# A graph network's last stage: the bias of each tile's normalisation formed on GpSimd instead of VectorE

## What is computed

```python
def _layernorm(x, axis=-1, eps=1e-05):
    m = jnp.mean(x, axis=axis, keepdims=True)
    v = jnp.var(x, axis=axis, keepdims=True)
    return (x - m) / jnp.sqrt(v + eps)
...
        out = node_feat + out
        mean = out.mean(axis=0)
        var = jnp.mean(jnp.square(out - mean), axis=0)
        out = (out - mean) * jax.lax.rsqrt(var + EPS) * gamma + beta
        return out
...
    x = _layernorm(x + _L1_gnn_ref(x, edge_attr_512, src, dst, ...), axis=-1)
```

## Time and profile before

| | us |
|---|---|
| median of 3 runs | 1352.58 (1351.42 to 1354.11) |
| span of the profiled execution | 1351.3 |
| GpSimd's first gather of the last stage starts | 1206.03 |
| gather 11 / gather 78 (the last) start | 1226.25 / 1336.43 |
| last normalisation starts with two others at | 1347.08 |

### The profile page before, as it was taken

The page is one execution under the profiler, slowest core; times in us unless marked ns, Lnnn a source line. Parts: engine busy times, 40 slices in busy tenths (PEclk is TensorE's granted clock), DMA queues, the critical chain, the costliest instruction groups (busy, mean ns, idle before and its releaser), DMA issues. The chain is left out here.

```text
span 1351.3 us, 21818 instructions
## 1 busy us (share of the span) xinstructions
PE 1282.1 (95%) x6374; PEld 1029.1 (76%) x6374; DVE 1075.9 (80%) x2074; ACT 638.2 (47%) x1243; POOL 817.3 (60%) x752
## 2 busy tenths in 40 slices
PE   7989989999999699999999999999999999979887
PEld 5768768888888588888888888888888888754333
DVE  6577649999999225888889988888888888977887
ACT  3576637888888212333233223322332233257777
POOL 3667346776765542566655666666666565467775
PEclk9999989999999799999999999999999999879999
DMA  8889767888885514444444344444444443759886
GB/s 279 287 280 297 259 203 261 255 257 276 259 261 188 187 47 110 141 131 129 97 135 128 127 126 131 139 135 137 133 140 140 140 140 94 258 175 368 272 283 228
DMA packets 128299, 257.93 MB, mean 191 GB/s; under 512 B 21459, under 2 KB 21907, under 8 KB 128114
## 3 DMA queue, kind: packets, MB, share of 16 engines
q1 hardware_dynamic: 97490, 175.31, 39.8%
q0 software_dynamic: 29920, 80.38, 20.6%
q10 hardware_dynamic: 832, 1.57, 0.3%
HBM read 197.18 MB, written 73.60 MB: 200 GB/s over the span
## 5 line engine op out<-in xcount | busy, mean ns | idle before, releaser
L208 PE MATMUL ps<-w_lo,w_hi 128*128 128x512 f32 (+2 forms) x1140 | 416.3, 365 | 3.6 <-DVE w_lo L1430 1.4
L210 PE MATMUL ps<-w_hi 128*128 128x512 f32 (+2 forms) x1140 | 410.7, 360 | 0.0
L209 PE MATMUL ps<-w_hi,w_lo 128*128 128x512 f32 (+2 forms) x1140 | 410.2, 360 | 0.0
L208 PEld LDWEIGHTS ps<-w_lo,w_hi 128*128 128x128 f32 x1140 | 217.5, 191 | 36.1 <-DVE w_lo L1512 1.9
L210 PEld LDWEIGHTS ps<-w_hi 128*128 128x128 f32 x1140 | 217.0, 190 | 32.4
L209 PEld LDWEIGHTS ps<-w_hi,w_lo 128*128 128x128 f32 x1140 | 217.8, 191 | 29.8
L1268 POOL TENSOR_TENSOR acc_x<-acc_x,node_rows 128x512 f32<-128x512 f32 x72 | 114.8, 1594 | 85.8 <-DMA node_rows<-x_table 81.5
L923 POOL TENSOR_TENSOR node_y<-node_z,node_x 128x512 f32<-128x512 f32 x79 | 102.7, 1300 | 74.0 <-DVE node_agg L1021 39.5
L208 PE MATMUL ps<-w_lo,agg_hi 128*128 128x512 f32 x316 | 132.8, 420 | 1.1 <-DVE agg_lo L992 1.1
L210 PE MATMUL ps<-w_hi,agg_hi 128*128 128x512 f32 x316 | 125.7, 398 | 0.0
L209 PE MATMUL ps<-w_hi,agg_lo 128*128 128x512 f32 x316 | 125.2, 396 | 0.0
(11 more groups left out here) (271 smaller groups left out, 2878.7 us busy)
## 6 DMA issues: line engine op xcount, KB each, us to landing
node_x<-in_x SPq DMA_DIRECT2D x79, 256.0 KB, 4.1
x_table<-node_x SPq DMA_DIRECT2D x79, 256.0 KB, 2.4
node_rows<-x_table SPq DMA_DIRECT2D x79, 256.0 KB, 8.4
coef_all<-coef_table SPq DMA_DIRECT2D x38, 512.0 KB, 7.6
edge_part<-part SPq DMA_DIRECT2D x40, 256.0 KB, 4.4
out_dram<-rows_over_w_lo SPq DMA_DIRECT2D x40, 256.0 KB, 5.7
node_x<-in_ea SPq DMA_DIRECT2D x38, 256.0 KB, 4.3
msg_table<-dst_rows_and_msg SPq DMA_DIRECT2D x38, 256.0 KB, 5.0
```

The source lines that it names most:

```text
L208: pe.matmul(to, left[0], right[1], start=first, stop=False, skip_group_check=onto)
L209: pe.matmul(to, left[1], right[0], start=False, stop=False, skip_group_check=onto)
L210: return pe.matmul(to, left[0], right[0], start=False, stop=last, skip_group_check=onto)
```

## The change

VectorE no longer forms the biases. GpSimd does, in a new third part of its loop: in step k, behind gather k and the multiplication of tile k - 4, it forms both biases of the pair that ends with tile k - 10 (`SHIFT` = 10). It raises a semaphore of its own, `bias_ok`, by one for each tile, and ScalarE's normalisation waits for that instead of `scale_ok`, which VectorE now raises only for the reciprocals. `pair_ends` is the test for the end of a pair, taken out into a function.

```diff
-    PAIR, NORM = 8, 11
+    PAIR, SHIFT, NORM = 8, 10, 11
...
+        def pair_ends(j):
+            return 0 <= j < NT and (j % 2 == 1 or j == NT - 1)
...
-        for k in range(NT + LATE):
+        for k in range(NT + SHIFT):
...
             j = k - LATE
-            if j >= 0 and by_pool(j):
+            if 0 <= j < NT and by_pool(j):
...
+            j = k - SHIFT
+            if pair_ends(j):
+                m, n = j // 2 * 2 % RM, j % 2 + 1
+                pool.wait_ge(scale_ok, j // 2 + 1)
+                for i in range(m, m + n):
+                    nc.gpsimd.tensor_scalar(bias[:, i, :], mv[:, i, 0:1], rstd[:, i, :], -1.0, ALU.mult, ALU.mult).then_inc(bias_ok, 1)
...
-                act.wait_ge(scale_ok, 3 * (j // 2) + 2 + j % 2)
+                act.wait_ge(bias_ok, j + 1)
...
-            if pair:
-                dve.wait_ge(scale_ok, done // 2 * 3 + 1)
-                for i in range(m, m + n):
-                    v.tensor_scalar(bias[:, i, :], mv[:, i, 0:1], rstd[:, i, :], -1.0, ALU.mult, ALU.mult).then_inc(scale_ok, 1)
```

More of the change, by code:

```diff
@@ L1894, in finish_stage @@
         u_before = [landed(NT - 1 - s, 0, 0, 4) for s in range(4)] + [32 * ET // 4] * 2 + [32 * NB // 2] * 2
-        us_ok, pool_ok, sum_ok, stat_ok, root_ok, scale_ok, norm_ok = (sem(n) for n in (
-            "fin_u_scaled_in_psum", "fin_u_scaled_by_pool", "fin_y_summed", "fin_stat", "fin_root_ok", "fin_scale_ok", "fin_norm"))
+        us_ok, pool_ok, sum_ok, stat_ok, root_ok, scale_ok, bias_ok, norm_ok = (sem(n) for n in (
+            "fin_u_scaled_in_psum", "fin_u_scaled_by_pool", "fin_y_summed", "fin_stat", "fin_root_ok", "fin_scale_ok", "fin_bias_ok", "fin_norm"))
+        def pair_ends(j):
+            return 0 <= j < NT and (j % 2 == 1 or j == NT - 1)
         open_ok = g.open_ok
@@ L2081, in vector_program @@
             done = k - PAIRED
-            pair = 0 <= done < NT and (done % 2 == 1 or done == NT - 1)
-            m, n = done // 2 * 2 % RM, done % 2 + 1
-            if pair:
+            if pair_ends(done):
+                m, n = done // 2 * 2 % RM, done % 2 + 1
                 dve.wait_ge(root_ok, done // 2 + 1)
```

## The result

The changed kernel takes 1429.41 us (median of 4 runs, 1428.20 to 1432.74), the kernel before 1352.26 us (4 runs): a ratio of 1.0565, with a 95% interval of 1.0547 to 1.0583. It is 5.65% slower. The forecast was 1423.5 us, with a range of 1405 to 1438.

The account below looks back on a forecast made before the run. The prediction took GpSimd, near its packed pace, to bound the last stage, and a new mutual wait with ScalarE to decide: 70.4 us of loop + 0.5 at the end on 1352.6 gives 1423.5 us, range 1405 to 1438.

Parts of the forecast that it names:

- What bounds the kernel: Last stage: GpSimd runs within 2.5% of its packed pace, 110.18 us for 67 tiles against a floor of 107.5.
- Part 1: VectorE loses 79 operations, 12.7 us; counted as nothing on the path, at the very best 2.7 us.
- Part 2: GpSimd gains 79 operations of one element per partition, two after each gather of an odd step, 0.30 us each.
- d: Time of one small bias operation on GpSimd, taken as 0.30 us; 0.40 by the Trainium skill's ratio.
- Part 3: Odd steps: ScalarE's normalisation waits for a bias behind gather k, which waits for ScalarE's copy; +70.4 us.
- The two pairs of steps: Time from gather k to gather k + 2: 4.52 + d us without a multiplication, 5.65 + d with one.
- The rival of the cheaper handover: Same loop, but a gap of 0.30 us instead of 0.81 from copy to gather: 1406 us, chance 8%.
- the clock costs nothing in the middle: At TensorE's low clock, nine products take 6.9 us, less than the 10.8 us of four tiles in the loop.
- the load rival: Normalisation doesn't wait for gather k, so no loop; GpSimd bound by its load: +15 us, 1368 us, chance 4%.
- The end: From gather 78 to the end of the last normalisation, now 12.75 us: 0 to 2 us more, 0.5 taken.
- the upper bound: The 2 us at the end of the stage, expected if TensorE has fallen to its low clock by then.
- The sum: 70.4 us in the loop + 0.5 at the end = 70.9 us, added to 1352.6: 1423.5 us, 5.2% slower.

Follow-up runs that it names:

- load_alone: Kernel before, biases still on VectorE, plus two small GpSimd operations on a spare tile behind every second gather, nobody waiting for them: 1361.4 us.
- no_mult: Kernel before with all multiplications on VectorE, none on GpSimd: 1351.1 us.
- pool_eighth: Kernel before with one tile of eight multiplied on GpSimd instead of one of four: 1352.1 us.
- no_bias: Kernel before with the 79 biases left out; the normalisation takes a constant: 1351.2 us.
- load_and_wait: Kernel before, biases still on VectorE, plus two small GpSimd operations behind every second gather, for which ScalarE's normalisation also waits: 1427.7 us.
- bias_first: Changed kernel with the two biases of a step ahead of its gather instead of behind it: 1384.1 us.
- shift9: Changed kernel with SHIFT set from 10 to 9, so a pair's biases stand behind the gather and multiplication of the even step before: 1383.3 us.
- two_more_ahead: Changed kernel with two more small GpSimd operations at each pair, between the gather and the first bias: 1444.8 us.
- two_more_behind: Changed kernel with two more small GpSimd operations at each pair, behind the second bias: 1431.8 us.
- last_on_vector: Changed kernel with the biases of tiles 66 to 78 staying on VectorE: 1421.3 us.
- pair_no_mult: Kernel before with one VectorE operation for the two biases of a pair and all multiplications on VectorE: 1349.9 us.

## Why the prediction was right, point by point

**What bounds the kernel.** GpSimd near its packed pace: read rightly from its timeline, and load_alone confirms that load on it has a price, 11.6 us. That it alone sets the pace was too strong, as no_mult and pool_eighth showed. The prediction didn't need more than the first half.

**Part 1, VectorE's relief counts as nothing.** Right: 0.14% at best in no_bias, nothing in load_and_wait.

**Part 2, the price of the operation.** d was taken as 0.30 us, the trace has 0.270. The estimate of 0.40 by the Trainium skill's ratio (GPSIMD Engine Reference, section on performance versus the Vector engine) was further off: here the ratio to VectorE's 0.202 us is 1.34, not 1.96. For this operation of one element a ratio measured on long ones was no guide; the short copies of the earlier trace rows were.

**Part 3, the wait makes a loop.** Right, and shown by five runs: the place of the biases is worth 47 us (bias_first, shift9), two operations cost 15.4 us on one side of the biases and 0.1 us on the other (two_more_ahead, two_more_behind), and the operations with the wait reproduce the change without any relief of VectorE (load_and_wait). The two pairs of steps took 4.84 and 5.97 us for 4.82 and 5.95. For the whole stretch 180.6 us were forecast and 182.39 measured. The difference has these terms: gathers of the even steps take 1.05 us, not 1.00 (33 x 0.05 = 1.6 us), and one gather, at 1353.11, starts 1.1 us late. The smaller d gives 34 x 0.03 = 1.0 us back. The rival of the cheaper handover is out, since it is 0.81 or 0.82 us in every turn of the loop. That the clock costs nothing in the middle was right too: a turn has the same length at 0.70 and at 0.99. Three details were off. The idle time in front of the gathers of even steps was put at some 1.5 us and is 1.90, where the prediction's own terms give 3.22 + 0.30 - 1.04 - 0.03 - 0.60 = 1.85. The normalisations' waits for the bias are 35, not 40. And the load rival took it that a bias ahead of gather k would leave no loop; bias_first still has one, through gather k - 1, and takes 1384 us instead of 1368.

**The end.** This term was mis-sized: 0.5 us taken, at most 2 allowed, and 5.0 us measured (19.89 against 14.87). It has two parts. The last normalisation starts 2.1 us later behind gather 78 than before, just past the upper bound (1423.33 - 1410.61 and three normalisations in 2.10, 14.82 us against 12.75). The step that failed is that VectorE would have the statistics of those tiles done by then. Normalisation 68 starts 2.63 us behind gather 78, not 0.57 (2.4 forecast), and VectorE's statistics of tile 73 start at 4.19 us, not 2.12, because VectorE's multiplication of tile 75 stands in front of them and waits for the bank that normalisation 68 frees. The delay of 2.1 us then stays to the last tile. It is not the clock, which the prediction made the condition for the upper bound: in load_and_wait the granted clock is 1.00 over these 12.8 us, and the last normalisation starts 12.77 us behind gather 78, where the changed kernel has 12.72.

The other 2.9 us stand at the end of the program, which the prediction hadn't looked at: GpSimd's closing `DRAIN`, hidden before. last_on_vector takes 4.5 of these 5.0 us back.

**The sum.** 70.9 us were forecast; the medians differ by 77.2 us, the profiled spans by 79.2. Of the 79.2 us, 72.2 are in the loop and 5.0 at the end. The remaining 2.0 lie ahead of gather 11, of which 1.75 ahead of gather 0, where the two programs have the same instructions; in the other runs gather 0 starts anywhere from 1200.0 to 1210.3 us. The prediction set the profiled span 1.3 us under the median; the runs of the changed kernel show 2.1 to 2.2 us between an execution's time and its span, so the profile of before was likely one of its slower runs. That changes nothing in the difference.

**No version beats both.** pair_no_mult has the lowest median of the complete kernels, 0.15% under the kernel before, with an interval that includes no change.

## What to carry to other kernels

When a step moves to another engine, write down what stands ahead of it in that engine's order, and what that waits for in turn. Here the bias stood behind a gather that waited for a copy on the very engine that waited for the bias, and 20 us of small operations became 72 us of turn-taking. Loads say nothing about this: in the profile both engines have idle time, and each names the other as the one that ended it. The distance in steps between a producer and its consumer is worth checking before what the operation itself costs: one step of distance was worth 47 us, the operations 12. No run tried a distance at which the loop is gone altogether.

## What the runs showed of the hardware

An operation of VectorE that reads two tensors from SBUF (128x2, two operands) can take 1.90 us instead of 0.14 when GpSimd multiplies 128x512 in SBUF, and ends with it. The Trainium skill, SBUF — State Buffer, section on the two separate sides, describes an exclusive lock on a pair of ports that such operations share with GpSimd, which goes to whichever starts first and blocks the other whole. The blocking agrees. That the first to start wins doesn't show in the records: VectorE's starts at 1274.91, GpSimd's multiplication at 1275.51, and VectorE's still ends last. What decides whether an operation is caught isn't settled: the eleven start 0.27 to 0.60 us ahead of a multiplication, yet one that starts 0.90 us ahead (1338.82) and one that starts 0.03 us ahead (1347.52) take 0.14. The form with the second operand given as one value per partition, as in the kernel before, reads two operands from SBUF as well and never took over 0.215 us there. In load_alone 25 of these operations start while GpSimd multiplies, and none takes over 0.21 us.

A gather on GpSimd starts 0.81 or 0.82 us behind the end of the copy for which it idles, in every turn of the loop, and 0.30 us behind another gather when nothing is awaited; a small operation on GpSimd behind a gather starts 0.03 to 0.04 us after it. And GpSimd's closing `DRAIN` ends 6.93 to 6.96 us behind its last operation, in all fourteen kernels: the kernels whose GpSimd works to the last tile end 2.9 to 3.6 us later for it.
